# Row sums and blend factors of windowed attention: one group per head in place of one per two heads

## What is computed

```python
for i in range(0, S, half):                 # half = 256, window = 512
    scores = jnp.einsum('bhqd,bkd->bhqk', Qw, Kw) * scale
    attn = jax.nn.sigmoid(scores)
    attn = attn / jnp.sum(attn, axis=-1, keepdims=True)
    wout = jnp.einsum('bhqk,bkd->bhqd', attn, Vw)
    ...
        alpha = jnp.linspace(0.0, 1.0, oe - i)
        blended = (1.0 - alpha) * out[:, :, i:oe] + alpha * wout[:, :, :oe - i]
```

## Time and profile before

| | us |
|---|---|
| time before, median of 3 runs | 2738.78 |
| lowest, highest | 2734.57, 2919.33 |
| the profiled execution, its own time | 2735.53 |
| its span on the slowest core (core 0) | 2733.7 |
| the spans of the 8 cores | 2710.4 to 2733.7 |
| PE busy in that span | 1979.1 (72%) |
| ACT, DVE busy | 655.8 (24%), 584.5 (21%) |

### The profile page before, as it was taken

How to read it: one execution, slowest core, us unless ns; L and a number is a source line. 1 busy time by engine, 2 the same in 40 slices (tenths; PEclk the granted TensorE clock), 3 DMA queues, 4 the chain that set the end, 5 groups by cost and what they waited for, 6 DMA issues and landing times.

```text
span 2733.7 us, 49232 instructions; the slowest of 8 cores (2710.4 to 2733.7 us)
## 1 busy us (share of the span) xinstructions
PE 1979.1 (72%) x20000; PEld 1701.4 (62%) x20000; DVE 584.5 (21%) x1624; ACT 655.8 (24%) x1143; POOL 101.8 (4%) x82
## 2 busy tenths in 40 slices
PE   1357999999977777775599999911214999999500
PEld 0247999999755555554588888811213888888400
DVE  2421222222133333333000000034343000000244
ACT  3650111111344444442011111142332111111111
POOL 1000000000000000000000000000000000000000
PEclk9999999999877777777799999955556999999855
DMA  9721456446000000000855646321134456465133
GB/s 207 191 89 32 63 72 84 64 63 85 9 2 2 2 2 2 2 2 8 88 77 71 85 63 93 47 62 48 45 74 67 64 73 88 64 81 80 62 154 154
DMA packets 228585, 178.94 MB, mean 65 GB/s; under 512 B 18960, under 2 KB 222736, under 8 KB 222736
## 3 DMA queue, kind: packets, MB, share of 16 engines
q0 software_dynamic: 217568, 113.35, 32.1%
q1 hardware_dynamic: 10800, 62.45, 6.1%
HBM read 263.97 MB, written 25.17 MB: 106 GB/s over the span
## 4 chain that ended last, share of the span: by engine, by line
PE 66%; DVE 11%; ACT 9%; issue 7%; DMA 6%; DVEq 1%; ACTq 0%; SPq 0%; POOL 0%; POOLq 0%
PE ps_all L655 16%; PE ps_all L770 16%; PE ps_all L443 16%; PE ps_all L542 8%; DVE bn L263 5%; DMA xstage<-x_ext 3%; PE ps_all L494 3%; ACT sig L508 2%; DMA out<-outstage 2%; DVE outstage L796 1%; ACT xt_stage L282 1%; DMA slab<-woT 1%; PE ps_all L295 1%; PE ps_all L679 1%; ACT outstage L282 1%
## 5 line engine op out<-in xcount | busy, mean ns | idle before, releaser
L655 PE MATMUL ps_all<-slab,attn_T 128*128 128x256 bf16 x4096 | 449.2, 273 | 38.8 <-DMA slab<-woT 38.8
L443 PE MATMUL ps_all<-slab,ln1T_own 128*128 128x256 bf16 x4096 | 469.6, 273 | 0.6 <-ACT krT L374 0.6
L770 PE MATMUL ps_all<-slab,ln2T 128*128 128x256 bf16 x4096 | 462.5, 273 | 0.1
L655 PEld LDWEIGHTS ps_all<-slab,attn_T 128*128 128x128 bf16 x4096 | 401.6, 98 | 86.3 <-issue 38.9
L770 PEld LDWEIGHTS ps_all<-slab,ln2T 128*128 128x128 bf16 x4096 | 401.4, 98 | 47.3 <-issue 0.2
L443 PEld LDWEIGHTS ps_all<-slab,ln1T_own 128*128 128x128 bf16 x4096 | 396.3, 98 | 45.1 <-issue 0.8
L542 PE MATMUL ps_all<-v_sb,sig 128*128 128x128 bf16 x2048 | 232.2, 244 | 92.4 <-DVE bl L586 88.3
L508 ACT ACTIVATE sig<-ps_all,kbias_s 128x512 bf16<-128x512 f32 x384 | 225.2, 721 | 272.5 <-PE ps_all L494 272.5
L542 PEld LDWEIGHTS ps_all<-v_sb,sig 128*128 128x128 bf16 x2048 | 223.4, 125 | 99.9 <-issue 99.9
L551 PE MATMUL ps_all<-onesc,sig 128*128 128x1 bf16 x2048 | 228.7, 189 | 0.0
L551 PEld LDWEIGHTS ps_all<-onesc,sig 128*128 128x128 bf16 x2048 | 192.9, 101 | 0.0
(11 more groups left out here) (86 smaller groups left out, 1473.7 us busy)
## 6 DMA issues: line engine op xcount, KB each, us to landing
slab<-wqT POOLq DMA_DIRECT2D x16, 2048.0 KB, 17.4
slab<-woT POOLq DMA_DIRECT2D x16, 2048.0 KB, 15.4
slab<-baseT POOLq DMA_DIRECT2D x16, 2048.0 KB, 14.1
xstage<-x_ext SPq DMA_DIRECT2D x12, 2048.0 KB, 15.3
out<-outstage SPq DMA_DIRECT2D x8, 2048.0 KB, 6.3
xre<-x_ext POOLq DMA_DIRECT2D x8, 1024.0 KB, 10.1
x_scratch<-x1b SPq DMA_DIRECT2D x8, 1024.0 KB, 4.3
x1re<-x_scratch SPq DMA_DIRECT2D x8, 1024.0 KB, 5.3
```

The lines of the kernel that those rows point to most:

```text
L443: return e.matmul(reg, ln1T_own[:, d, t * 128:(t + 1) * 128], slabs[par][:, d, :], start=(d == 0), stop=(d == 31))
L655: return e.matmul(reg, attn_T[:, d, t * 128:(t + 1) * 128], slabs[par][:, d, :], start=(d == 0), stop=(d == 31))
L770: return e.matmul(reg, ln2T[:, d, t * 128:(t + 1) * 128], slabs[par][:, d, :], start=(d == 0), stop=False)
```

## The change

The row sums, the factors and the blends are worked head by head. The loop over two halves and two heads in each becomes one loop over four heads. Each head takes a bank of the ring of its own for its row sums and uses 4 columns of it; its chain on DVE (reciprocal and product of 128x4 instead of 128x8, then the head's two pairs of `fb1` and `fb2`) is emitted right behind the head's matmuls. The number and the order of the matmuls stay as they are, and so do the blends. Reciprocals and products go from 64 to 128 each, and the ring serves 16 banks a step in place of 14. The layout of the alpha weights, which the host fills in, follows the new order of columns. The core of the diff:

```diff
-        for half in range(2):
-            rbank, rbw = sc_ring.acquire()
-            w_first = [(s_sig, c_sig_all)] + rbw
...
-            for h4 in (2 * half, 2 * half + 1):
-                bk = 2 + (h4 & 1)
+        for h4 in range(4):
+            bk = 2 + (h4 & 1)
             rbank, rbw = sc_ring.acquire()
...
+                    col = win * 2 + qh
+                    for jj in range(4):
+                        j = 2 * win + jj
+                        w0 = ()
+                        if first:
+                            w0 = list(w_first) + list(av_free[h4 & 1]) + rbw
+                        elif win == 0 and qh == 0 and jj == 0:
+                            w0 = list(av_free[h4 & 1]) + rbw
...
+                        rst = (win == 0 and qh == 0 and jj == 0)
+                        rlast = (win == 1 and qh == 1 and jj == 3)
...
+                        P.op("tensor", fr, inc=(s_av if rlast else None))
+                        if rlast:
+                            r_end = s_av.n
+                        first = False
+            w1d = s_av.n
+            uoff = h4 * 4
             P.op("vector", lambda e, rbank=rbank, uoff=uoff: e.reciprocal(
-                    ur16[:, uoff:uoff + 8], rbank[:, 0:8]),
+                    ur16[:, uoff:uoff + 4], rbank[:, 0:4]),
                  waits=[(s_av, r_end), (s_u, s_u.n)], inc=s_chain)
             c_rc = s_chain.n
             sc_ring.release_last((s_chain, c_rc))
             P.op("vector", lambda e, c=c, uoff=uoff: e.tensor_mul(
-                    u16[:, uoff:uoff + 8], ur16[:, uoff:uoff + 8],
-                    alpha_s[:, c * 16 + uoff: c * 16 + uoff + 8]),
+                    u16[:, uoff:uoff + 4], ur16[:, uoff:uoff + 4],
+                    alpha_s[:, c * 16 + uoff: c * 16 + uoff + 4]),
                  waits=[(s_chain, c_rc)], inc=s_u)
...
-            for h4 in (2 * half, 2 * half + 1):
-                bk = 2 + (h4 & 1)
-                for qh in range(2):
-                    colp = uoff + (0 * 2 + qh) * 2 + (h4 & 1)
-                    colc = uoff + (1 * 2 + qh) * 2 + (h4 & 1)
+            for qh in range(2):
+                colp = uoff + 0 * 2 + qh
+                colc = uoff + 1 * 2 + qh
...
+                P.op("vector", fb1,
+                     waits=[(s_u, c_u), (s_av, w1d)] + list(bl1_free.get(bp, [])),
+                     inc=s_chain)
...
+            av_free[h4 & 1] = [(s_bl, s_bl.n)]
```

More of the change, by code:

```diff
@@ L518, in emit_rav_main @@
         binfo = []
-        for half in range(2):
-            rbank, rbw = sc_ring.acquire()
-            w_first = [(s_sig, c_sig_all)] + rbw
[L522 to L525, removed]
-            r_end = 0
-            w1ds = {}
-            for h4 in (2 * half, 2 * half + 1):
-                bk = 2 + (h4 & 1)
-                for win in (0, 1):
-                    for qh in range(2):
[L532 to L559, removed]
@@ new lines, in emit_rav_main, with fa, fr @@
+        w_first = [(s_sig, c_sig_all)]
+        if first_u[0]:
+            w_first.append((s_const, CONST_N))
+            first_u[0] = False
+        first = True
+        for h4 in range(4):
+            bk = 2 + (h4 & 1)
+            rbank, rbw = sc_ring.acquire()
+            r_end = 0
+            w1d = 0
+            for win in (0, 1):
+                for qh in range(2):
+                    reg0 = (win * 2 + qh) * 128
+                    col = win * 2 + qh
[6 more added lines that the diff above has]
+                            w0 = list(av_free[h4 & 1]) + rbw
+                        def fa(e, j=j, h4=h4, qh=qh, c=c, jj=jj, reg0=reg0, bk=bk, sbuf_sig=sbuf_sig):
+                            return e.matmul(ps[bk][:, reg0:reg0 + 128],
+                                            sbuf_sig[:, j, h4, qh * 128:(qh + 1) * 128],
+                                            v_sb[:, 2 * c + j, :],
+                                            start=(jj == 0), stop=(jj == 3))
+                        P.op("tensor", fa, waits=w0,
+                             inc=(s_av if (win == 1 and jj == 3) else None))
+                        rst = (win == 0 and qh == 0 and jj == 0)
+                        rlast = (win == 1 and qh == 1 and jj == 3)
+                        def fr(e, j=j, col=col, qh=qh, h4=h4, st=rst, lst=rlast,
+                               sbuf_sig=sbuf_sig, rbank=rbank):
+                            return e.matmul(rbank[:, col:col + 1],
+                                            sbuf_sig[:, j, h4, qh * 128:(qh + 1) * 128],
+                                            onesc[:, :], start=st, stop=lst)
+                        P.op("tensor", fr, inc=(s_av if rlast else None))
[4 more added lines that the diff above has]
+            uoff = h4 * 4
@@ new lines, in emit_rav_main, with fb1, fb2 @@
+            for qh in range(2):
+                colp = uoff + 0 * 2 + qh
+                colc = uoff + 1 * 2 + qh
+                bp = (h4 & 1) * 2 + qh
+                def fb1(e, qh=qh, h4=h4, colp=colp, bp=bp, bk=bk):
+                    return e.tensor_scalar(bl1[bp][:, :],
+                                           ps[bk][:, (0 * 2 + qh) * 128:(0 * 2 + qh) * 128 + 128],
+                                           u16[:, colp:colp + 1], None, ALU.mult)
+                P.op("vector", fb1,
+                     waits=[(s_u, c_u), (s_av, w1d)] + list(bl1_free.get(bp, [])),
+                     inc=s_chain)
+                c_t1 = s_chain.n
+                p2, w2 = bl2_ring.acquire()
+                def fb2(e, qh=qh, h4=h4, colc=colc, p2=p2, bp=bp, bk=bk):
+                    return e.scalar_tensor_tensor(bl2[p2][:, :],
+                                                  ps[bk][:, (1 * 2 + qh) * 128:(1 * 2 + qh) * 128 + 128],
+                                                  u16[:, colc:colc + 1],
+                                                  bl1[bp][:, :],
+                                                  ALU.mult, ALU.add)
+                P.op("vector", fb2,
+                     waits=[(s_chain, c_t1)] + w2, inc=s_bl)
+                bl1_free[bp] = [(s_bl, s_bl.n)]
+                binfo.append((qh, h4, p2, s_bl.n))
@@ L853, in _host_inputs @@
                 a = np.ones(256, dtype=np.float32)
-            for half in range(2):
+            for h4 in range(4):
                 for qh in range(2):
-                    for h4b in range(2):
-                        alpha_a[:, c * 16 + half * 8 + (0 * 2 + qh) * 2 + h4b] = 1.0 - a[qh * 128:(qh + 1) * 128]
-                        alpha_a[:, c * 16 + half * 8 + (1 * 2 + qh) * 2 + h4b] = a[qh * 128:(qh + 1) * 128]
+                    alpha_a[:, c * 16 + h4 * 4 + 0 * 2 + qh] = 1.0 - a[qh * 128:(qh + 1) * 128]
+                    alpha_a[:, c * 16 + h4 * 4 + 1 * 2 + qh] = a[qh * 128:(qh + 1) * 128]
         in_maps.append({
```

## The result

The changed kernel takes 2694.3 us (median of 10 runs) against 2735.2 us for the kernel before (median of 10 runs). The ratio is 0.9841, with a 95% interval of 0.983 to 0.9853, so 40 to 47 us less. The forecast was 2694. In some executions the cores of a die run at a lower clock from start to end; the ratios leave such runs out, the medians don't (without them they are 2692.0 and 2734.9), and where they were the majority the lowest time is given.

The account below looks back on a forecast made before the run. PE and ACT were taken to pace the attention step by turns, with PE's stall for DVE's chain also lowering its clock. Gains of 38 us over 32 steps plus 3 us in the last two gave 2694 us, range 2664 to 2722.

Parts of the forecast that it names:

- What bounds the stage: Attention stage: PE and ACT pace each 16.95 us step by turns; PE's 2.73 us wait for DVE also lowers its clock.
- The prices: One attention step: head 2 may start at 4.17 us, head 3 at 6.47, last matmul 7.74 at full clock against 9.66.
- The stall is cut in two, not removed: AV matmuls: two PE waits a step, 1.57 and 1.00 us at full clock, 55 to 80 us in sum, not 88.
- The clock: Attention steps: 15 in 100 at full clock, 65 falling before head 3, 20 low from head 0; mean gain 1.12 to 1.2 us.
- The last steps: Last two attention steps, without scores between: PE waits for a one-head chain, 1.5 us less each, 3 us in all.
- The rest of the step: Scores and transposes after the four heads: stays at 7.29 us, the score tiles' wait for row-sum banks costing nothing.
- The fast rival: Attention stage: the clock stays up in the shorter gaps, 70 us gained, 2665 us; chance 15 in 100.
- The low-clock rival: Attention stage: clock low in most steps from head 0 on, only 14 us gained, 2722 us; chance 20 in 100.
- The slower rival: Attention stage: DVE's chain becomes the bound, break-even at 2.87 us a head; time 2790 us; chance 4 in 100.

Follow-up runs that it names:

- e3: The changed kernel with two more 128x4 products in each head's DVE chain; 2739.6 us, ratio 0.999 to the kernel before.
- e1: The changed kernel with filler matmuls, results never read, in PE's gaps ahead of heads 2 and 3; 2686.7 us, ratio 0.980 to the kernel before.
- e2: The kernel before with 28 filler matmuls, results never read, in PE's stall ahead of head 2; 2719.5 us, ratio 0.991.
- e4: The kernel before, chains for two heads kept, with a PSUM bank for each of the four heads' AV results; 2636.5 us, ratio 0.961.
- e6: e4 with one 128-column filler matmul ahead of each score tile; 2620.5 us, ratio 0.958 to the kernel before.
- e5: The changed kernel, a chain for each head, with the four banks of e4; 2668.0 us (lowest), no ratio, too few runs.
- e9: The changed kernel with 704 filler matmuls, results never read, at the very end of PE's list; 2707.5 us (lowest), ratio 0.990 to the kernel before.
- e7: e6 with the loads of the output projection's first two weight slabs issued earlier on POOL's queue; 2574.7 us, ratio 0.938 to the kernel before.

## Why the prediction was right

- **What bounds the stage.** Right. PE's wait for the blends and its clock set the step; e3, e1 and e2 each move one of the two and the time follows.
- **The prices.** At a full clock, reciprocal 0: predicted at 1.64 us, measured 1029.42 - 1027.78 = 1.64. Head 2: 4.17 against 4.25. DVE's pitch a head: 2.30 against 2.27, since the 4-column reciprocal takes 177 ns and not 208 (mean of core 0's 128). Head 3: 6.47 against 6.51. Last matmul at a full clock: 7.74 against 7.78; at the low clock in head 3: 8.53 against 1020.36 - 1011.78 = 8.58:

```profile
1018.30 0.27 PE L541 MATMUL ps_all<-v_sb,sig 128*128 128x128 bf16 x1 [0.82 <-DVE bl L584]
...
1020.36 0.21 PE L551 MATMUL ps_all<-onesc,sig 128*128 128x1 bf16 x1
```

- **The stall is cut in two, not removed.** Right: 70.0 us in 60 waits on core 0, within the 55 to 80 foreseen, and e3 shows that the second gap is a chain of two.
- **The clock.** I took 15 of 100 steps at a full clock, 65 low before or in head 3, 20 low from head 0. Read from each head's matmul starts, it was 19, 75 and 6. The steps of each kind took nearly what I had for them: 14.9, 15.9 and 16.5 us, against 14.9, 15.8 and 16.6. The mean step went from 17.01 to 15.71 us, a gain of 1.30 where I had 1.2: this is the term that was mis-sized, by 3 us over the stage. The shares were a guess from few rows. (The clock of 0.7 that I read off the page's tenths is 0.79 in the stretch.)
- **The last steps.** They gave the 3 us: 1.2 more than a usual step gains at the start of the last one, and 1.9 from the last AV matmul to the last transpose (4.9 to 3.0). But the projection's first matmul did not come sooner after the last AV matmul (39.8 and 39.3 us in the mean), so these 1.9 us did not reach the total. With the two errors of opposite sign, and runs that spread over 7 us, it is luck that the median agrees with the forecast to a third of a microsecond. That it agrees to a few is not.
- **The rest of the step.** Right: the wait of score matmuls for a reciprocal, which I had costed at nothing, is 0.6 us in all on core 0.
- **The fast rival** is refuted as the common case: with gaps of 1.52 and 0.82 us the clock comes down in four steps of five, and with fillers in the gaps (e1) in fewer than one of five. It did show which prize lay there: e1 reaches it in the stage.
- **The low-clock rival** happens in 6 steps of 100 here. Its mechanism, a fall while PE runs scores at ACT's pace, is the one that holds e4 back, and e6 removes it.
- **The slower rival** has its break-even near where it was put: at 2.80 us a head, against 2.87, e3 ends at 0.9994.

What I didn't see is how near the other sign was: with two more banks the same change costs 34 us (e5).

## What to carry to other kernels

When an engine waits for a buffer, first ask whether more buffers can be had before making the chain that frees them shorter: splitting the chain gave 41 us here, and two idle banks gave 103. A stall on TensorE is to be priced with the clock behind it; matmuls whose result nobody reads are a quick test of that share, and here even a usable means. A finer grain of a chain pays only while someone waits for its first piece; past that, its extra instructions lengthen whatever waits for its last.

## What the runs showed of the hardware

- TensorE's granted clock went from 2.4 to 1.2 GHz in a loop with gaps of 1.5 and 0.8 us and a head of matmuls between them (changed kernel), and also while score matmuls ran at ACT's pace (two of 256 columns each 0.57 us, no gap above 0.27 us for the 4 us ahead of the fall, e4). One 128-column matmul more for each tile kept it up (PEclk 0.90 to 0.99, e6).
- Steps of the changed kernel that do the same work take 14.9 us where the clock holds and 15.9 where it falls ahead of head 3 or in it, often one after the other.
- 704 matmuls at the end of PE's program delay the landing of the first stage's input tiles by some 11 us (e9), 384 by some 7 (e6, e7).
